# Latent attention layers: when a couple of batches gets its second queries and its odd values

## The reference, cut to what matters

```
h = concatenate([x, latents], axis=1)                 # 128 context rows and 128 latent rows per batch
q = (latents @ q_w + q_b).reshape(b, 128, 16, 32)
kmat, v = split of (h @ kv_w + kv_b)                  # 256 keys and values per batch
attn = softmax(where(mask, q kmat / 32, -inf))
attn_out = (attn v) @ out_w + out_b + residual
out = gelu(rmsnorm(attn_out) @ mlp_w1 + mlp_b1) @ mlp_w2 + mlp_b2 + residual
```

## Time and profile before

| what | value |
|---|---|
| median of 3 runs | 2559.47 us (2557.16 to 2562.12) |
| the profiled execution's own time | 2562.53 us |
| its span, first to last instruction | 2560.7 us |
| PE busy | 2452.8 us, 96% of the span |
| DVE, ACT, POOL busy | 1231.4, 1085.6, 1120.2 us |
| mean granted TensorE clock | 0.982 |

### The profile page before, as it was taken

The page is one execution under the profiler, slowest core; times in us unless marked ns, Lnnn a source line. Parts: engine busy times, 40 slices in busy tenths (PEclk is TensorE's granted clock), DMA queues, the critical chain, the costliest instruction groups (busy, mean ns, idle before and its releaser), DMA issues.

```text
span 2560.7 us, 48767 instructions
## 1 busy us (share of the span) xinstructions
PE 2452.8 (96%) x18464; PEld 2053.4 (80%) x18464; DVE 1231.4 (48%) x3296; ACT 1085.6 (42%) x3712; POOL 1120.2 (44%) x1972
## 2 busy tenths in 40 slices
PE   7999998999999999998888999999999999899999
PEld 6888886888888878886777788888888888788887
DVE  4555655332224667766666332243455556432332
ACT  4555554111114787777767111111455555311111
POOL 2453545600053787778876630033344443730000
PEclk9999999999999999998988999999999999999999
DMA  4111312211033233223443320122021111320100
GB/s 162 59 59 59 104 55 79 83 50 50 1 109 126 74 106 121 96 97 125 150 161 121 115 91 1 50 87 74 26 88 63 51 43 61 114 87 1 50 33 17
DMA packets 106774, 198.07 MB, mean 77 GB/s; under 512 B 8304, under 2 KB 35632, under 8 KB 103600
## 3 DMA queue, kind: packets, MB, share of 16 engines
q1 hardware_dynamic: 106544, 194.97, 23.1%
HBM read 136.22 MB, written 58.72 MB: 76 GB/s over the span
## 4 chain that ended last, share of the span: by engine, by line
PE 79%; ACT 11%; DVE 5%; POOL 3%; issue 1%; DMA 1%; SPq 0%; DVEq 0%; POOLq 0%
PE banks L326 70%; ACT plain_high L731 5%; PE banks L467 5%; PE banks L497 3%; ACT plain_low L731 2%; POOL plain_high L1342 2%; ACT plain_work L796 1%; DVE stats L1134 1%; PE banks L521 1%; ACT plain_work L715 1%; DVE plain_work L1149 0%; DMA plain_high<-attention_w 0%; DVE plain_high L1004 0%; ACT plain_low L715 0%; DVE rounded_low L1053 0%
## 5 line engine op out<-in xcount | busy, mean ns | idle before, releaser
L326 PE MATMUL banks<-rounded_work,rounded_low 128*128 128x512 f32 (+1 forms) x2688 | 534.3, 355 | 11.5 <-DVE rounded_low L1166 9.5
L326 PEld LDWEIGHTS banks<-rounded_work,rounded_low 128*128 128x128 f32 x2688 | 445.3, 198 | 76.8 <-issue 15.9
L982 ACT ACTIVATE plain_work<-banks,columns 128x512 f32<-128x512 f32 x192 | 132.4, 690 | 870.8 <-PE banks L326 870.8
L326 PE MATMUL banks<-rounded_work,rounded_high 128*128 128x512 f32 (+1 forms) x2400 | 483.4, 355 | 2.1 <-DMA rounded_work<-ctx_split 1.7
L326 PEld LDWEIGHTS banks<-rounded_work,rounded_high 128*128 128x128 f32 x2400 | 396.6, 191 | 68.2 <-issue 6.2
L1342 POOL TENSOR_SCALAR plain_high<-plain_high,inv_sum 128x128 f32<-128x128 f32 (+1 forms) x768 | 296.6, 409 | 317.5 <-DVE inv_sum L1026 317.2
L1318 DVE CAST rounded_work<-plain_work 128x512 fp32r<-128x512 f32 x192 | 105.3, 549 | 685.7 <-ACT plain_work L982 674.9
L326 PE MATMUL banks<-rounded_low,rounded_work 128*128 128x512 f32 x1728 | 414.9, 391 | 0.0
L326 PE MATMUL banks<-rounded_high,rounded_work 128*128 128x512 f32 (+1 forms) x1728 | 390.2, 377 | 0.0
L326 PEld LDWEIGHTS banks<-rounded_low,rounded_work 128*128 128x128 f32 x1728 | 321.6, 188 | 68.6 <-issue 2.8
L326 PEld LDWEIGHTS banks<-rounded_high,rounded_work 128*128 128x128 f32 x1728 | 309.1, 188 | 60.5 <-issue 1.4
(11 more groups left out here) (106 smaller groups left out, 3120.9 us busy)
## 6 DMA issues: line engine op xcount, KB each, us to landing
plain_work<-x SPq DMA_DIRECT2D x96, 256.0 KB, 3.2
plain_work<-mlp_w SPq DMA_DIRECT2D x96, 256.0 KB, 2.7
rounded_work<-ctx_split SPq DMA_DIRECT2D x16, 1024.0 KB, 6.0
u<-plain_work SPq DMA_DIRECT2D x48, 256.0 KB, 2.8
plain_work<-u SPq DMA_DIRECT2D x12, 1024.0 KB, 7.2
x<-plain_work SPq DMA_DIRECT2D x48, 256.0 KB, 2.3
plain_work<-attention_w SPq DMA_DIRECT2D x44, 256.0 KB, 2.6
ctx_split<-rounded_work SPq DMA_DIRECT2D x8, 1024.0 KB, 5.6
```

The lines of the kernel that those rows point to most:

```text
L326: mm = pe.matmul(dst, lhs(i), rhs(j), start=first and n == 0, stop=last and n == 2, skip_group_check=True)
L982: act.activation(gelu[:, j % 2, :], bank(key), ACT.Gelu_apprx_tanh, bias=col(y, 28 + j)).then_inc(evac_of(key), 1)
```

## The change

In both latent layers a couple gets its queries 1 and its values 1 and 3 in its own round 1 (between turn 0 and scores 2), instead of at the end of the couple before. The rest of the next couple's projections comes one or two quarters later: keys' 0 and 1 after attend 1 (they were after attend 0), queries' 0 after turn 2 (after turn 1), values' 0 and 2 after attend 2, keys' 2 and 3 together after attend 3. The out of the last odd batch and the turning of x' move from round 0 to round 1. In couple 7 the turned MLP rows and the outs move with them, and the out of batch 14 comes before turn 3. `pe_attend` waits for the two value blocks of its own batch only. ACT and DVE follow the same order. GpSimd's norm 2 now stands ahead of the root of the last odd batch and of tiles 8 and 9. SP stores the even row and loads the next one at the head of its loop.

```diff
-                for i in range(4 if y.kind == LATENT else 1):
+                for i in (b, 2 + b) if y.kind == LATENT else (0,):
                     wait_evac(pe, ("V", y.n, p, i))
...
             pe_scores(pe, y, 0, 0)
-            pe_keys(pe, y, 0, 2)
-            pe_keys(pe, y, 0, 3)
-            pe_queries(pe, y, 0, 1)
-            for i in range(4):
+            for i in (2, 3):
+                pe_keys(pe, y, 0, i)
+            for i in (0, 2):
                 pe_values(pe, y, 0, i)
             for p in range(PAIRS):
                 more = p + 1 < PAIRS
                 pe_scores(pe, y, p, 1)
                 pe_turn_probs(pe, y, p, 0)
-                if more and y.n:
+                pe_queries(pe, y, p, 1)
+                pe_attend(pe, y, p, 0)
+                pe_values(pe, y, p, 1)
+                pe_values(pe, y, p, 3)
+                pe_scores(pe, y, p, 2)
+                pe_turn_probs(pe, y, p, 1)
+                if not more:
+                    pe_turn_u(pe, M[y.n], 0, 0)
+                    pe_turn_u(pe, M[y.n], 0, 1)
+                elif y.n:
                     pe_turn_x(pe, y, p + 1)
                 if p:
                     pe_out(pe, y, 2 * p - 1)
-                pe_attend(pe, y, p, 0)
+                pe_attend(pe, y, p, 1)
                 if more:
                     pe_keys(pe, y, p + 1, 0)
                     pe_keys(pe, y, p + 1, 1)
...
                 else:
                     pe_turn_u(pe, M[y.n], 0, 2)
                     pe_turn_u(pe, M[y.n], 0, 3)
+                pe_scores(pe, y, p, 3)
+                pe_turn_probs(pe, y, p, 2)
+                if more:
+                    pe_queries(pe, y, p + 1, 0)
                 pe_attend(pe, y, p, 2)
                 if more:
+                    pe_values(pe, y, p + 1, 0)
+                    pe_values(pe, y, p + 1, 2)
+                    pe_scores(pe, y, p + 1, 0)
+                else:
+                    pe_out(pe, y, 2 * p)
+                pe_turn_probs(pe, y, p, 3)
+                if more:
+                    pe_out(pe, y, 2 * p)
+                pe_attend(pe, y, p, 3)
+                if more:
+                    pe_keys(pe, y, p + 1, 2)
                     pe_keys(pe, y, p + 1, 3)
...
                 pool_norm(pool, y, p, 1)
+                pool_norm(pool, y, p, 2)
                 if p:
                     pool_root(pool, y, 2 * p - 1)
                 if not more:
                     pool_mlp_tiles(pool, y, 8, 10)
-                pool_norm(pool, y, p, 2)
                 pool_bias(pool, y, 2 * p)
...
                 more, far = p + 1 < PAIRS, p + 2 < PAIRS
+                if p:
+                    sp_store_u(sp, y, 2 * p - 2)
+                    sp_next_hidden(sp, y, 2 * p)
                 if not more:
                     sp_first_rows(sp, y)
```

More of the change, by code:

```diff
@@ L560, in pe_latent @@
                     pe_keys(pe, y, p + 1, 1)
[L561 to L564, removed]
-                else:
[L566 to L571, removed]
+                else:
+                    pe_turn_u(pe, M[y.n], 0, 2)
+                    pe_turn_u(pe, M[y.n], 0, 3)
                 pe_scores(pe, y, p, 3)
@@ L868, in inputs @@
                 def inputs():
-                    if more and y.n:
+                    if not more:
+                        act_turn_u(act, M[y.n], 0, 0)
+                        act_turn_u(act, M[y.n], 0, 1)
+                    elif y.n:
                         act_x(act, y, p + 1, 0)
                         act_x(act, y, p + 1, 1)
-                    elif more:
+                    else:
                         act_stage(act, p + 1)
-                act_round(act, y, p, 1, (p, 0), inputs)
+                act_round(act, y, p, 1, (p, 0), nothing)
+                act_queries(act, y, p, 1)
                 act_heads(act, y, p, 0)
+                act_values(act, y, p, 1)
+                act_round(act, y, p, 2, (p, 1), inputs)
+                act_heads(act, y, p, 1)
                 if more:
@@ L894, in act_latent @@
                     act_turn_u(act, M[y.n], 0, 3)
+                act_round(act, y, p, 3, (p, 2), nothing)
+                if more:
+                    act_queries(act, y, p + 1, 0)
                 act_heads(act, y, p, 2)
                 if more:
-                    act_keys(act, y, p + 1, 3)
-                if not more:
+                    act_values(act, y, p + 1, 0)
+                else:
                     act_warm(act, 1 if y.n == 0 else 5, ACT.Gelu_apprx_tanh)
@@ L1177, in dve_latent @@
             dve_keys(dve, y, 0, 3)
-            dve_queries(dve, y, 0, 1)
-            dve_values(dve, y, 0, 1)
+            dve_values(dve, y, 0, 2)
             for p in range(PAIRS):
                 more = p + 1 < PAIRS
-                dve_values(dve, y, p, 3)
                 def inputs():
-                    if more and y.n:
+                    if not more:
+                        dve_turn_u(dve, M[y.n], 0, 0)
+                        dve_turn_u(dve, M[y.n], 0, 1)
+                    elif y.n:
                         dve_x(dve, y, p + 1, 0)
                         dve_x(dve, y, p + 1, 1)
-                    elif more:
+                    else:
                         dve_stage(dve, p + 1)
-                dve_round(dve, y, p, 1, (p, 0), inputs)
+                dve_round(dve, y, p, 1, (p, 0), nothing)
+                dve_queries(dve, y, p, 1)
+                dve_heads(dve, y, p, 0)
+                dve_values(dve, y, p, 3)
+                dve_round(dve, y, p, 2, (p, 1), inputs)
                 if p:
                     dve_out(dve, y, 2 * p - 1)
-                dve_heads(dve, y, p, 0)
+                dve_heads(dve, y, p, 1)
                 if more:
```

56 lines of the change are left out of this document (12 added, 44 removed).

## The result

The changed kernel takes 2565.84 us in the median of 9 runs (2561.97 to 2571.09), the kernel before 2559.63 us in 9 runs beside it. The ratio is 1.0028, 95% interval 1.0019 to 1.0037: slower by about 7 us by the ratio, 6.2 us by the medians. I had forecast 2558.5 us and "no difference", with 0.17 on slower; the time lies 1.3 us above the range.

What follows compares the result with a forecast made beforehand. PE, busy for 96% of the span, was taken as the bound. The terms -1.0 (layer 0), -0.05 (layer 3) and +0.3 (mask) gave -0.75 us, clock at 0: 2558.7, rounded to 2558.5 us; range 2551 to 2564.5 us.

Steps and rivals of the forecast that it cites:

- 0.3 us for all together: Middle couples: the mask ahead of round 3's maxima costs 0.3 us over fourteen couples, bounds 0 and 10.2 us.
- third rival: Slower: attend 2 late in each middle couple, mask and keys' 1 ahead of round 3's maxima; up to 2568.7 us; chance 0.10.
- bound of 0.73 us per couple: Middle couples: the largest mask, 1.38 us, would stick out of the 0.65 us cover before attend 2 by 0.73 us.
- -1.0 and -0.05: Couple 7, scores 1 to the MLP: 1.0 us won in layer 0 and 0.05 us in layer 3.
- a term put at nothing: PE's lower clock, put at 0 in the sum, with 2.9 us either way.
- From norm 3's start to the MLP 11.1 us: Couple 7: turn 3, uncovered attend 3 and out 15 sum to 11.1 us after norm 3 starts at 36.3 us.
- fourth rival: Slower: the clock falls over out 15 and the MLP's first matmuls, 2 x 2.9 us, 2564.3 us; chance 0.06.
- Middle couples: Couples 1 to 6: the 0.22 us wait before keys' 0 stays; gain 0, bounds 0 and 1.33 us.
- SP's new order: Row store and next row's load ahead of `sp_c` cost 0; cover some 6 us; rival that `XC` comes late 0.04.
- Couple 0: Attend 0's 2.22 us wait moves to attend 1, and keys' 0 keeps its own wait; gain 0.
- The second rival: Faster: tiles 8 to 11 do not hold norm 3; couple 7 6.4 and 5.4 us shorter, 2547.7 us; 0.12, half of it 0.08.
- the term of the clock in couple 0: Couple 0: 24 matmuls at the low clock, 8.62 us against 5.72; put at 0 with 2.9 us either way.

Runs made afterwards that it cites:

- experiment 1: Changed kernel with the next couple's mask moved behind the maxima, reciprocals and copies of round 3: 2562.96 us, ratio 1.0017 to the kernel before.
- 2: Changed kernel, mask left in place, GpSimd's bias add of the even batch moved ahead of norm 2: 2563.23 us, ratio 1.0015 to the kernel before.
- experiment 8: Changed kernel with the mask behind round 3's maxima and couple 7 alone in the order before: 2559.42 us, ratio 1.0000 to the kernel before.
- 6: Changed kernel, mask behind round 3, tiles 8 to 11 behind norm 3 (first kernel): 2555.12 us, 0.9993; also turned rows 2, 3 before attend 2: 2551.31 us, 0.9977.
- experiment 5: Tiles 8 to 11 behind norm 3 of couple 7: in the changed kernel 2555.43 us, ratio 0.9988; in the kernel before 2548.30 us, ratio 0.9971.
- 4: Changed kernel with the out of batch 14 put back behind turn 3 in couple 7: 2565.70 us, ratio 1.0030 to the kernel before.
- 7: Unread identity transposes filling PE's gaps in couple 7: changed kernel 2562.77 us, ratio 1.0024; kernel before with tiles 8 to 11 behind norm 3 2548.54 us, 0.9971.
- the last kernel of 8: Changed kernel, mask behind round 3's maxima, couple 7 in the order before, tiles 8 to 11 behind norm 3: 2551.53 us, ratio 0.9967 to the kernel before.

## Why the prediction was wrong

**The direction fell, by two terms of the sum.** The loss is 7 us; 0.0011 to 0.0013 of the ratio, some 3 us, go with the mask (experiments 1 and 2), and the other 0.0017, some 4 us, with couple 7 (experiment 8). Each step alone is about as large as its intervals, and those of neighbours touch. With the tiles late the mask's return does not show in the time at all (0.9993 against 0.9988, experiments 6 and 5). That the two are the whole rests on 8 ending at 1.0000 and on the rows, which give 2.3 us and 3.5 us for the same two places.

**The mask, "0.3 us for all together".** This step failed: the rows give 2.3 us in its place. It was the third rival's mechanism, to which I gave 0.10, but in the six middle couples of layer 0 alone, not in fourteen. The step was wrong twice.
- Its duration: I took the median of all 24 instructions, 0.33 us. That mixes layers and shapes: 0.33 us is what most of the eight uint8 masks of layer 1 take. Of the 14 masks in couples 0 to 6 of the latent layers, six took 0.28 us, and the other eight, one in layer 0 and all seven in layer 3, took 0.60 or 0.61 us. The row of before would have shown it, 128x256 int32 beside the eight operations of norm 2:

```profile
1831.00 0.60 DVE L1128 TENSOR_SCALAR plain_work<-plain_work 128x256 bf16<-128x256 int32 x1
```

In the new place it takes 0.77 us in layer 0. GpSimd's bias add of 1.28 us came to lie over the mask, behind norm 2 and the root, whose order the change had turned round. I had looked for what queues behind the mask on DVE, not for what GpSimd does at that moment. In every pair of rows the mask ends 0.14 or 0.15 us after the GpSimd instruction under way when it began: 118.65 after 118.51 us in the changed kernel, 119.55 after 119.40 in experiment 1.
- Its cover: I counted the whole 115.79 to 116.44 us as cover. 0.37 us of it are the way from a copy to its attend, as the new wait shows, so only 0.28 us were free. Maxima that start 0.7 us later, 2.19 us after the scores against the 1.49 of before, overrun that by about 0.4 us, and 0.38 us is what each couple lost. The bound of 0.73 us per couple was above it; the middle of my estimate was not near.

The Trainium skill has the rule for this ("SBUF — State Buffer", section "Who interferes with whom"): a VectorE instruction in a two-port mode, which `tensor_scalar` can be, and a GpSimd instruction lock each other out of a shared port pair for the whole instruction, whichever began first. The trace agrees: 0.76 us for work of 0.28 us, with its end tied to GpSimd's end. That the mask ran in such a mode no row shows.

**Couple 7, "-1.0 and -0.05".** This failed too: it measured +1.4 and +2.1 us. The chain up to norm 3 was right: root 13, the load of tile 8, four splits, norm 3. Every link is in the rows, and experiment 5 shows it sets the end. What was off is its size, and behind norm 3 the clock, a term put at nothing.
- Norm 3 starts 36.9 us after scores 1 in both layers, not 36.3; root 13 ends at 24.75 us, not 24.2, since norm 2, behind which it stands, starts 6.84 us after its scores (413.25 us), 1.8 us later than norm 1 in the kernel before (5.02 us after scores 1), where I had added 1.3. From there on each interval is as forecast (3.27 us to tile 8, 8.89 on to norm 3). Before it stood at 26.14 + 8.75 = 34.9 us: 2.0 us lost.
- "From norm 3's start to the MLP 11.1 us" became 12.9 us in layer 0. 1.6 us of the 1.8 are out 15 at the granted clock of 0.50, 4.42 us against the 2.84 us that I copied from the earlier trace rows. In layer 3 it is 4.23 us. I had this as the fourth rival, at 0.06, with 2.9 us a layer, twice what it cost, and left it out of the sum as a chance. No run shows the 0 that the sum took for the clock where idle time only moves; here it was 1.6 and 1.4 us. The slow out 15 came in both layers of the changed kernel, of experiments 1 and 2 and of the first kernel of 6, and in one layer of each kernel of 5. With out 14 behind turn 3 (4), with the turned rows moved (6) and with the gaps filled (7) out 15 ran at the full clock in both. The place of out 14 is not the whole reason: in the last kernel of 8, which has it behind turn 3, out 15 was slow in layer 0 (4.44 us). So what moving out 14 away saves behind norm 3 is 13.49 - 12.90 = 0.6 us in layer 0 and nothing in layer 3 (12.56 to 12.60 us), not 2.4.
- Together: 2.0 - 0.6 = +1.4 us in layer 0, +2.1 in layer 3.

**What held.** Middle couples: 0.22 us stays, and layer 3 has no idle time. SP's new order made nothing late. Couple 0: attend 0 starts without a wait, attend 1 has one of 2.19 us and keys' 0 one of 0.71 us, the two waits of the earlier trace rows, moved on as forecast. Attend 2 of couple 7 waits 3.32 us where "some 3" was forecast, turn 2 not at all for GpSimd. One line was wrong: turn 3 waits only 1.89 us for norm 3, less than the 2.66 of before, because out 14 in front of it ran slowly (4.82 us) and filled the gap.

**The second rival** (couple 7 really shorter) fell as stated, since the tiles do hold norm 3. Taken as an edit it is right: put behind norm 3 they give 7 us to the kernel before and 10 to the changed one. That version, or the one of the last run, beats both kernels: ratios 0.9971 and 0.9967.

**What stays open.** Why out 15 meets the low clock in one order and not in another is shown only as far as idle time in front of it goes; filling the gaps brought the clock back but no time that can be measured. The profiled executions differ by 8.3 us. 5.8 of them are the two places, 2.0 lie in couple 0 of layer 0 ahead of keys' 0, most of it at the start (scores 0 took 1.68 us against 1.01 before; the first 24 matmuls behind them took 7.89 us, and 5.74 in the changed kernel with late tiles, whose code is the same there), and 0.5 between the layers. That is as far as the one profile goes; the 1 us between the rows (5.8 us) and the ratio (7 us) stays open.

## What to carry to other kernels

When an instruction moves to a new place, look at what the other engine that shares its path to memory runs at that moment after the change, above all when the same edit reorders that engine's queue: a median over all occurrences prices the old neighbours, and mixes layers and shapes. Cover for a wait is what is left after the signal's own way, here 0.37 of 0.65 us; read it from a place where the consumer already waits. And at a layer's end, follow the chain that sets it before moving work that is off it: here four tile splits in a queue were worth more than the whole reordering.

## What the runs showed of the hardware

- A DVE `tensor_scalar` of 256 elements, int32 to bf16, takes 0.28 us alone. If a GpSimd `tensor_tensor` of 128x512 is under way for at least 0.2 us more, it ends 0.14 to 0.15 us after that one, so its length is what is left of the other: 0.37, 0.76 to 0.78 and 1.24 us in the rows above.
- The clock in couple 0, where the code is the same in all changed versions, differs from one profile to the next: the keys behind the stage (L326 after L1105) took 8.51 us in the changed kernel's profile, 6.59 in the one with late tiles and 5.73 in the one with the mask back. Two profiles can so differ by 2.8 us for no reason that the edits show. The timeline of PE with the mask back, to be read against the 8.62 us of the earlier trace rows:

```profile
55.92 5.73 PE L326 MATMUL banks<-rounded_work,rounded_low 128*128 128x512 f32 x24 [0.75 <-DVE rounded_work L1105]
```

- That was the term of the clock in couple 0, which I had put at 0 with 2.9 us either way; the profiles of before and after (8.62 and 8.51 us) and these two fit it.
